# Half of the expert products moved from the first attention's row maxima to the second attention's, wide mixing blocks there, and one subtraction handed from VectorE to GpSimd

## The reference, cut to what matters

```python
x = x + proj(attention0(group_norm(x)))              # 8 heads of 32 channels, every token sees all
t = tokens(x)                                        # (8, 1024, 256)
t = t + attention1(layer_norm(t)) @ W_O + b_O        # 8 heads, causal
n = layer_norm(t)
sel = sigmoid(n @ expert_sel.T)                      # 32 experts of 64 hidden units
sel_val, sel_idx = top_k(sel, 2)
w = scatter(sel_val at sel_idx)                      # (tokens, 32), two not zero
h = relu(einsum('td,edh->teh', n, keys))
t = t + einsum('teh,te,ehv->tv', h, w, values)
```

## Time and profile before

| | us |
|---|---|
| median of 3 runs | 3903.73 (3895.03 to 3910.25) |
| profiled execution, its own time | 3897.4 |
| its span in the trace | 3895.7 |
| PE busy | 3380.4 (87%) |
| DVE busy | 2022.0 (52%) |
| ACT busy | 1670.6 (43%) |
| POOL busy | 421.5 (11%) |
| mean granted TensorE clock | 0.892 of full |

### The profile page before, as it was taken

How to read it: one execution, slowest core, us unless ns; L and a number is a source line. 1 busy time by engine, 2 the same in 40 slices (tenths; PEclk the granted TensorE clock), 3 DMA queues, 4 the chain that set the end, 5 groups by cost and what they waited for, 6 DMA issues and landing times.

```text
span 3895.7 us, 54844 instructions
## 1 busy us (share of the span) xinstructions
PE 3380.4 (87%) x18386; PEld 1841.5 (47%) x18386; DVE 2022.0 (52%) x2825; ACT 1670.6 (43%) x2604; POOL 421.5 (11%) x539
## 2 busy tenths in 40 slices
PE   5898799987998879988799888998889988899779
PEld 2343464445634356343563445534465344554347
DVE  6434583356823568235672447624575254843544
ACT  1453335543364433644236343463434634345334
POOL 0000030001300013000230002200032000310005
PEclk7797899988999789988899898997889978999789
DMA  3011340114402043020530205202142022511125
GB/s 98 1 44 33 87 140 25 44 33 114 132 6 60 18 127 120 9 57 17 141 111 17 58 19 145 90 17 60 29 142 82 17 60 46 148 58 33 45 52 167
DMA packets 151948, 263.13 MB, mean 68 GB/s; under 512 B 26832, under 2 KB 28880, under 8 KB 151504
## 3 DMA queue, kind: packets, MB, share of 16 engines
q1 hardware_dynamic: 151632, 259.15, 24.6%
HBM read 145.80 MB, written 9.44 MB: 40 GB/s over the span
## 4 chain that ended last, share of the span: by engine, by line
PE 69%; DVE 13%; ACT 7%; issue 6%; SPq 3%; DMA 2%; DVEq 0%; POOL 0%; ACTq 0%; POOLq 0%
PE ps_acc L583 10%; PE ps_two L688 8%; PE ps_acc L592 8%; PE ps_one L535 7%; DVE tops L1050 7%; PE ps_two L652 6%; PE ps_one L537 5%; PE ps_one L536 5%; PE ps_one L688 3%; PE ps_acc L535 3%; PE ps_acc L536 3%; PE ps_acc L537 3%; SPq L448 2%; ACT stacks L840 2%; ACT probs L857 2%
## 5 line engine op out<-in xcount | busy, mean ns | idle before, releaser
L1050 DVE TENSOR_REDUCE tops<-ps_two 128x2 bf16<-128x1024 f32 (+3 forms) x896 | 964.4, 1112 | 431.8 <-PE ps_two L652 253.8
L857 ACT ACTIVATE probs<-ps_two 128x1024 f32<-128x1024 f32 (+1 forms) x704 | 642.3, 961 | 287.9 <-PE ps_two L688 220.4
L652 PE MATMUL ps_two<-stacks 32*128 32x512 f32 (+3 forms) x1792 | 426.9, 508 | 175.7 <-DVE tops L1050 135.4
L688 PE MATMUL ps_two<-stacks 97*128 97x512 f32 (+3 forms) x1408 | 462.7, 439 | 63.8 <-ACT probs L857 34.3
L583 PE MATMUL ps_acc<-probs,v_sb 128*32 128x512 f32 (+3 forms) x3584 | 474.8, 605 | 0.0
L510 POOL TENSOR_TENSOR nat<-expert_sb,nat 128x256 fp32r<-128x256 f32 x512 | 382.1, 747 | 644.1 <-ACT nat L801 546.7
L592 PE MATMUL ps_acc<-probs,ones 128*32 128x512 f32 (+3 forms) x3584 | 451.3, 578 | 0.0
L688 PEld LDWEIGHTS ps_two<-stacks 97*128 97x128 f32 x1408 | 250.1, 196 | 333.4 <-issue 187.9
L652 PEld LDWEIGHTS ps_two<-stacks 32*128 32x128 f32 x1792 | 172.4, 204 | 456.3 <-DVE tops L1050 230.6
L801 ACT CAST nat<-expert_sb 128x256 fp32r<-128x256 f32 x256 | 103.1, 406 | 616.3 <-DVE probs L1146 531.8
L516 POOL TENSOR_TENSOR act_lo<-xn,act_hi 128x2048 fp32r<-128x2048 f32 x8 | 36.1, 4509 | 2822.7 <-ACT act_hi L907 2822.7
(11 more groups left out here) (127 smaller groups left out, 4476.2 us busy)
## 6 DMA issues: line engine op xcount, KB each, us to landing
stacks<-nat SPq DMA_DIRECT2D x792, 128.0 KB, 2.4
expert_sb<-experts_dram SPq DMA_DIRECT2D x256, 256.0 KB, 2.8
probs<-gates_dram SPq DMA_DIRECT2D x512, 128.0 KB, 3.0
x_in<-x_in_dram SPq DMA_DIRECT2D x9, 1024.0 KB, 5.0
out_dram<-x_res SPq DMA_DIRECT2D x16, 512.0 KB, 2.9
probs<-mats_dram SPq DMA_DIRECT2D x1, 2048.0 KB, 9.3
gates_dram<-w_turn SPq DMA_DIRECT2D x64, 16.0 KB, 1.6
sel_w<-sel_dram SPq DMA_DIRECT2D x1, 32.0 KB, 8.3
```

The costliest lines, as they stand in the source:

```text
L652: mm = pe.matmul(acc[:, HALF * e:HALF * e + n_keys], q_st[rows, g, j, P * i:P * i + P], k_st[rows, g, j, HALF * kh:HALF * kh + n_keys], st ...
L688: mm = pe.matmul(at[:, a:HALF], k_st[0:MID + 1, g, j, P * k:P * k + P], q_st[0:MID + 1, g, j, HALF * hf + a:HALF * hf + HALF], start=True, ...
L857: done(act.activation(probs[:, n % 2, per * i:per * i + per, a:HALF], acc[:, :, a:HALF], ACT.Exp, scale=SCALE), s + (i,))
L1050: done(dve.reduce_max(tops[:, kh, 2 * pr:2 * pr + 2, i], acc[:, :, 0:cols(st, i, kh)], AX_X), s)
```

## The change

The experts of token half 1 of the image before stay in the first attention; those of half 0 of the current image are done in its own second attention. So `logits`, `inputs` and `turn` exist per half and work on half the tokens (4 instead of 8 gate writes, 512 instead of 1024 tokens each). The first attention now spreads its 54 tops behind 16 ups; the second attention does the four groups of its mixing blocks without tops between those of group g, takes `norm`, `out(1, 0)` and `lna(1, 0)` among the tops of (1, 0, 1), and spreads the tops of (1, 1, 1) behind 16 ups between g and h. "head" gets these 16 ups too, and "last" keeps 16 of its 32. All mixing blocks of the second attention are wide. The lower part of the gated product is subtracted by POOL, as a third instruction of its queue for each up. Two waits are new: SP holds the gate loads of half 0 until the mixing of group g is done (they overwrite `probs`), and ACT's exponentials of the first two blocks of h wait for `down(0)`.

```diff
-    def experts_of(self, tops):
-
-        ups = [("up", hf, j) for hf in range(self.halves) for j in range(self.experts)]
-        steps = spread(ups, tops) if tops else ups
-        at = steps.index(("up", 0, self.experts - 1)) + 1
-        behind = at + 2 if tops else at
-        return steps[:at] + [("lower", 0)] + steps[at:behind] + [("down", 0)] + steps[behind:] + [("lower", 1)]
+    def experts_of(self, hf, tops):
+
+        ups = [("up", hf, j) for j in range(self.experts)]
+        return (spread(ups, tops) if tops else ups)
 
     def batch(self, experts):
         tops = rows_later(self.top(0, 0, 0) + self.top(0, 0, 1) + self.top(0, 1, 0) + self.top(0, 1, 1))
         if experts:
-            steps = self.qk(0, 1, [0]) + [("logits",)] + self.v(0)[2:] + self.qk(0, 1, [1]) + [("inputs",)]
-            steps += tops[:3] + [("turn",)] + tops[3:10] + self.experts_of(tops[10:])
+            steps = self.qk(0, 1, [0]) + [("logits", 1)] + self.v(0)[2:] + self.qk(0, 1, [1]) + [("inputs", 1)]
+            steps += tops[:3] + [("turn", 1)] + tops[3:10] + self.experts_of(1, tops[10:])
...
-        e, f, g, h = (self.mix(1, g, hf, hf == g) for hf in (0, 1) for g in (0, 1))
+        e, f, g, h = (self.mix(1, g, hf, True) for hf in (0, 1) for g in (0, 1))
         t = rows_later(self.top(1, 1, 0))
         steps += e[:1] + [("norm", 0, 1, 1)] + self.qk(1, 1, [0]) + [("div", 0, 1, 1), e[1], e[2], ("fin", 0, 1, 1)]
         steps += [e[3]] + t[:3] + self.out(0, 1) + t[3:8] + [("lna", 0, 1)] + t[8:]
         steps += f[:1] + [("norm", 1, 0, 0), ("lnb", 0, 1), f[1], f[2], ("parts", 1), ("div", 1, 0, 0)]
-        steps += self.qk(1, 0, [1]) + [("fin", 1, 0, 0)] + self.v(1)[2:]
-        steps += spread([f[3]] + self.qk(1, 1, [1]), rows_later(self.top(1, 0, 1)))
-        m = [g[1], ("div", 1, 1, 0), g[2], ("fin", 1, 1, 0)] + g[3:]
+        steps += self.qk(1, 0, [1]) + [("fin", 1, 0, 0)] + self.v(1)[2:] + [f[3]] + self.qk(1, 1, [1])
+        t = rows_later(self.top(1, 0, 1))
+        steps += [("norm", 1, 1, 0)] + t[:2] + [("div", 1, 1, 0)] + t[2:5] + [("fin", 1, 1, 0)] + t[5:9]
+        steps += self.out(1, 0) + t[9:14] + [("lna", 1, 0)] + t[14:]
+        steps += g[:2] + [("lnb", 1, 0), g[2], g[3], ("logits", 0), g[4], ("inputs", 0), g[5], ("turn", 0), g[6], g[7]]
         t = rows_later(self.top(1, 1, 1))
-        steps += g[:1] + [("norm", 1, 1, 0)] + spread(m[:-1], t[:-1]) + [m[-1], t[-1]]
-
-        steps += h[:1] + [("norm", 1, 0, 1), h[1], ("div", 1, 0, 1), h[2], ("fin", 1, 0, 1), ("stats",), h[3]]
-        steps += self.out(1, 0) + [("gn",), h[4], ("lna", 1, 0), h[5], ("split", 0), ("lnb", 1, 0), h[6], h[7]]
+        m = self.experts_of(0, t[2:])
+        steps += t[:2] + [("norm", 1, 0, 1)] + m[:3] + [("div", 1, 0, 1)] + m[3:7] + [("fin", 1, 0, 1)] + m[7:]
+
+        steps += h[:1] + [("down", 0), h[1], ("stats",), h[2], ("gn",), h[3], h[4], ("split", 0), h[5], h[6], h[7]]
         steps += [("norm", 1, 1, 1), ("div", 1, 1, 1)] + self.qk(0, 0, [0]) + [("fin", 1, 1, 1)] + self.v(0)[:2]
         steps += self.out(1, 1)
         steps += [("split", 1), ("lna", 1, 1)] + self.qk(0, 0, [1]) + [("lnb", 1, 1)]
         return steps
 
     def last(self):
-        return [("logits",), ("inputs",), ("turn",)] + self.experts_of([]) + [("down", 1)]
+        return [("logits", 1), ("inputs", 1), ("turn", 1)] + self.experts_of(1, []) + [("down", 1)]
...
-                        for i in range(TT):
-                            sp.dma_start(w_dram[:, P * i:P * i + P],
-                                         w_turn[E * (i % PH):E * (i % PH) + E, i // PH, :]).then_inc(gates_out, 16)
-                        hold(gates_out, "turn", sec.no["turn"][s], 16 * TT)
-                        for m in range(RING):
-                            load_gates(m)
+                        for i in range(PH):
+                            at = HALF * hf + P * i
+                            sp.dma_start(w_dram[:, at:at + P], w_turn[E * i:E * i + E, hf, :]).then_inc(gates_out, 16)
+                        hold(gates_out, "turn", sec.no["turn"][s], 16 * PH)
+                        if hf == 0:
+
+                            hold(mixed, "mix", sec.no["mix"][last_mix(sec, ("norm", 1, 0, NH - 1))])
+                        for j in range(RING):
+                            load_gates(hf, j)
...
+                        lower(hf, j, vals_up, vals_parts, C, vals_down)
+                        pool.wait_ge(gated_up, sec.value("up", sec.no["up"][s]))
+                        pool.tensor_tensor(gated_lo[:, j % 2, :], gated[:, j % RING, :], f(gated_hi[:, j % 2, :]),
+                                           ALU.subtract).then_inc(gated_down, 1)
...
+                            read(("out", 1, hf, CT - 1) if hf else ("up", hf, ET - 1))
...
+                        if s[1:4] == (1, 1, NH - 1) and k < 2:
+                            act.wait_ge(acc_read, sec.value("acc", sec.no["acc"][("down", 0)]))
...
-                def lower(m):
-
-                    dve.wait_ge(gated_up, sec.value("up", m + 1))
-                    dve.tensor_tensor(gated_lo[:, m % 2, :], gated[:, m % RING, :], f(gated_hi[:, m % 2, :]), ALU.subtract).then_inc(gated_down, 1)
...
-                        if j:
-                            lower(m - 1)
-                    elif kind == "lower":
-                        lower((s[1] + 1) * ET - 1)
```

182 lines of the change are left out of this document (96 added, 86 removed).

## The result

The changed kernel takes 4171.50 us (median of 4 runs, 4165.47 to 4189.36) against 3904.88 of the kernel before on the same chip (median of 4, 3895.03 to 3910.25): a ratio of 1.0688, 95% interval 1.0657 to 1.0720, slower. 4089 was forecast.

What follows compares the result with a forecast made beforehand. PE was taken to pace the first attention's ups, with 50 us per image lost in the second attention. 7 x (-23 + 50) + 50 - 47 = +192 on the profiled 3897.4 gave 4089 us, range 3955 to 4175.

Steps and rivals of the forecast that it cites:

- What bounds the kernel: PE paces the first attention's ups; 50 us per image are lost in the second attention, 22 of them to the clock.
- the second rival: Second attention absorbs the experts: PE stays fed, the clock rises to full, 31 of 50 us filled; 3841 us, chance 0.12.
- Term A: First attention, seven times: fewer logits, gate writes and 16 fewer ups, less 8 us for the clock; -23 us each.
- The count: First attention, first gate product to first mixing block: bank uses behind each up summed to 96.8 us at full clock.
- Term B: Second attention, eight times: 149 us replace 97.5 in most stretches, group h -1.3; +50 us each.
- the two projections of (1, 1, 1) come in at 1.5 each: Group f of the second attention: these two added at 1.5 us each, the stretch staying at 30 us.
- the price of `out` and `lna`: Tops of (1, 0, 1): PE's `out` at 3.0 us and `lna` at 2.0 stop the supply of tops; stretch 29 us.
- Term C: "last", once: shorter start -8.3, 16 ups leaving -43.5, POOL's pace and the end +5; -47 us.
- The moved subtraction: First attention: DVE's subtraction, taken over by POOL, would have fitted into DVE's gap; its removal costed at nothing.
- Wide blocks: Group f of the second attention: half the number of exponentials, saving some 3 us of PE and ACT.
- The better coupling: Rival: two banks let PE run ahead, first attention meets DVE's floor at -44 us; 3942 us, chance 0.14.
- GpSimd does not pace: Rival claimed GpSimd paces or blocks: second-attention ups lifted from 3.40 to 3.9 us, 56 more, 4145 us; chance 0.04.

Runs made afterwards that it cites:

- e10: Changed kernel with two unused 128-row products ahead of each third and later bank use before an up, first attention: 4098.32 us, ratio 1.0515.
- e4: Changed kernel with the score products of every top of the body's first attention given twice: 4235.29 us, ratio 1.0847.
- e9: Changed kernel with two extra 128-row, 512-column products ahead of every top of the body's first attention: 4218.58 us, ratio 1.0825.
- e1: Changed kernel with the projections of (1, 1, 1) moved behind the sixth top of (1, 0, 1): 4134.85 us, ratio 1.0595.
- e2: Changed kernel with each up's value products given out behind the next two tops: 4070.29 us, ratio 1.0457.
- e6: Changed kernel with the lower part of the gated product subtracted by DVE again: 4188.12 us, ratio 1.0721.
- e7: Kernel before with POOL subtracting the lower part of the gated product: 3919.73 us, ratio 1.0037.
- e3: Changed kernel with projections of (1, 1, 1) later and value products behind two tops: 4061.14 us, ratio 1.0405.
- e12: Kernel before with two extra 128-row products ahead of each of eight full-width tops of (1, 0, 1): 3893.22 us, ratio 0.9976.

## Why the prediction was right in its sign and 82 us short

**What bounds the kernel** held. The lost time of the second attention wasn't filled: g and the ups together went from 41.5 to 87.7 us, +46.2 against the forecast +48. Of the 58.7 us of the ups PE was busy for 53.5 in the pass shown, at a clock of 1.00, so there they run as PE-bound as in the forecast. The start of h lengthened as foreseen. PE's instructions are 18386 before and after: no work has gone, and what moved to a stretch in which PE already was the limit isn't hidden there. The 50 us of lost time that the prediction starts from are too many, though: its 22 are half of all the time at the lower level, and where PE stood idle that level costs nothing. The sum doesn't use them, only the second rival does.

**Term A, −23 forecast, −13.7 measured (65 us over seven passes). This is the larger miss, and its step is the size taken for the clock.** The coupling by two banks was right: in the pass shown the first gate product runs at 2075.53, 35.1 us into the pass against 41.4 before, and the waits are at the third and later bank uses. The count gave 96.8 us at full clock from the first gate product to the first mixing block. Measured are 2190.5 − 2075.5 = 115.0 (114.4 over the seven passes), so 18 and not 8 lie over it. Over the seven passes 58% of the key halves are slow, and the 12 products of such an up take 4.65 us on average where those of the others take 3.14. So I estimate 16 × 0.58 × 1.5 = 14 of these 18 as the clock's (13 to 16, by where the end of a key half is set). I had computed 9 from a mean clock of 0.84 and taken 8; the mean was 0.81, and the slow time fell on the long products of the ups rather than on waits, where it would have been hidden. e10 confirms it from the other side: at 0.93 the same distance is about 107.8 − 3.1 = 104.7, so 8 over the count, of which its 17% of slow key halves are 4.

The Trainium skill (TensorE: Matmul & The Clock Gate, What's actually happening) says that the clock is set by how busy the PE has been. For the direction the traces agree: the thinned stretch fell from 0.97 to 0.81 and the filled one came to 1.00. The busy share of the profile alone doesn't tell the clock, though: e4 raised it to 85%, and its clock was 0.78 in that window, and in the first ten tops 75% busy went with 0.61 in e4 and 69% with 0.94 in e9. The measurement decides.

**Term B, +50 forecast, +54.3 measured (30 us over seven passes). Two steps failed. The first is "the two projections of (1, 1, 1) come in at 1.5 each".** That is what they cost PE. Placed right behind those of (1, 0, 1), their copy on ACT waits for the DMAs that still read `nat`, and SP issues all 24 of both in a row, in 20.9 us. Behind this copy stand norm's copy, `div` and the reductions. I had asked which queue each moved step passes, for the ups, and not for the projections. The tops took 37.2 instead of the forecast 29; e1 took 4.0 of these 8.2 away. The second step is the price of `out` and `lna` in this stretch, 3.0 and 2.0, which holds at full clock: the rows show 5.1 and 3.65, 3.75 more, and the sixth pass, at 0.72, is 3.2 us shorter than the others. In the kernels here that don't touch this stretch it took between 33.9 us at a clock of 0.72 (e10) and 37.6 at 0.60 (e2). The two parts are read from different runs, so that they sum to 8 is no proof that they are all of it.

**"head"**: +49.8 against +50. **Term C** −55.7 against −47: I had GpSimd at 3.0 us an up with waits, and it ran at 2.72 without any, as fast as PE. The 5 us for that were not needed, and the start shrank by more.

Together 192 + 65 + 30 − 9 = 278, against 277 measured.

**The moved subtraction**, costed at nothing, is at most 17 us in either kernel (e6, e7), with opposite signs. **Wide blocks** were mis-sized only by being counted in f alone: g gains 4.3 more, which the tops behind f partly take back.

**The rivals.** The better coupling fell: the waits are where the count put them. That the second attention absorbs the experts fell with the 87.7 us. GpSimd does not pace: the last gate products of the second attention still follow each other by 3.4 us, a gate product of DVE takes 689 ns on average where it took 687 before, and e7 costs 0.4%.

Left open: why e3 gains less than its two parts, and why the clock in the tops (1, 0, 1) is 0.60 in most passes and 0.72 in others with the same work.

## What to carry to other kernels

Before work is moved out of a stretch to thin it, ask what the stretch was bound by: with two banks, each bank use beyond the second waits a full reduction, and halving the PE work between tops (128.2 to 117.7 us for half the ups) bought 8% of its time. Price the PE work that stays at the clock that a stretch with those waits gets, and remember that the lower level lands on the long products too. For every moved step look at the buffer that its first copy overwrites and at the transfers that still read it: the wait shows up several queues away, under another name.

## What the runs showed of the hardware that I had not expected

- The same number of added products had different effects on the granted clock: with each top's score products (32 rows) given twice, 0.81 stayed 0.81 over the seven passes; with two 128-row products of 512 columns per top it became 0.95. In the first ten tops it was 0.61 and 0.95, and not for the busy share alone: one pass had 0.61 at 75% busy, another 0.94 at 69%. The runs differ in the rows, but also in the numbers multiplied, and I haven't shown which of the two makes the difference.
- Products whose results nobody uses shortened the kernel: 73 us less in e10, where they stand in PE's waits, and 0.24% less than the kernel before in e12.
- GpSimd subtracts 128x512 in 1.29 us and two of 128x256 in 1.51, back to back without a gap: 2.72 for each up. DVE was lightly used beside it (15.88 of 66.5 us in "last").
